# The root's reciprocal of fifteen normalisations computed as a power of -0.5 on GpSimd

## The chip, the cores and the metric

One core of one Trainium2 chip. The metric is the device time of one execution of the program in microseconds; the kernel before takes 1572.85 us (median of 3 runs, 1572.19 to 1574.05).

## The reference

Four layers run one after the other on x (16 sequences of 100 rows of 256 numbers) and a context (16 sequences of 361 rows). All of it is in float32. Cut to the normalisations, which alone are touched:

```
# layer 0: self attention, cross attention, feed-forward (gelu), a layer norm behind each
x = ln(x + self_attention(x));  x = ln(x + cross_attention(x, ctx));  x = ln(x + ffn(x))
#   ln(x) = (x - mean(x)) * rsqrt(var(x) + 1e-5) * gain + bias
# layer 1: self attention, swiglu, cross attention, swiglu, with residuals and without norms
# layer 2: rms(x) -> gates, a recurrence over 100 steps, attention on ctx; rms again -> gelu ffn
#   rms(x) = x * scale * rsqrt(mean(x * x) + 1e-6)
# layer 3: attention of the result on ctx, tanh of a product, added to the hidden states
```

## The kernel before

Activations lie transposed in SBUF, 256 features as two chunks (`DC`) of 128 partitions, 1600 columns for the 16 sequences. The columns are taken in four groups (`NG` = 4) of `GB` = 4 sequences, 400 columns each. The attention stages are called s0, c0 (layer 0), s1, c1 (layer 1) and c2 (layer 2), the feed-forward stages f0, f1, f2 and ft; they run in the order s0, c0, f0, s1, f1, c1, f2, gates, c2, ft, and then layer 3.

There are five normalisations of four groups each, 20 "chains": n1 (behind s0), n2 (behind c0), n3 (behind f0), r1 (ahead of layer 2) and r2 (ahead of ft). The chain of a group is spread over the stages that follow it: a product with a matrix of 1/256 gives the mean (n1 to n3), VectorE subtracts it (`dve_center`), ScalarE squares (`act_square`), a product gives the variance in PSUM (`pe_var`), ScalarE computes Sqrt of variance plus a small constant into `T2` (`act_root`), VectorE takes the reciprocal in place and multiplies both chunks (`dve_scale`), and for n1 to n3 ScalarE applies gain and bias (`act_affine`).

Each engine runs one list of instructions in order; semaphores are counted and each wait names a point that another engine marks. In an attention stage the order within a sequence is a string of tokens (`ORDER`). For c0 it is

```
"c0": "T0 T1 T2 n0 P1 n1 R0 R1 V0 R2 R3 T3 V1 T4 R4 R5 T5 F T6 T7 F K0 V2 K1 F X p0"
```

T is a score product of the next sequence and its maxima on VectorE (bank freed when the maximum is taken), R are the score products of this one and ScalarE's exponential (`act_probs`), X turns the maxima and VectorE makes `max_rows` of them (`dve_rows`), which the next sequence's R0 needs; F is one step of the "fill", among it the chain of the group before. With three F in a sequence of c0, the variance product and `act_root` of a chain lie in the first F of the group's third sequence, and `dve_scale` in its second F, ahead of that sequence's X on VectorE. In a feed-forward stage a fill step follows each of the eight hidden chunks (`pe_up`, then `act_evac` with the gelu), before the two products of `pe_down` that read all eight.

GpSimd (`program_pool`) runs `pool_masks` (one or two products of the queries with 0/1 columns; T needs the first, `qh`), in s0 also `pool_allowed`, in c1 and c2 sums of probabilities, and in c2 the steps of the recurrence. In c0 the masks of a sequence b wait for the last scores of sequence b - 3. T of sequence b + 1 is issued within sequence b.

ScalarE holds one set of function tables at a time; where the next function is in another, an ACT_TABLE_LOAD stands in its list.

Of the kernel before, what the change touches and what calls it, by code (L numbers as in the profile page):

```python
# [10 lines left out]
ACT = mybir.ActivationFunctionType  # L11
ALU = mybir.AluOpType
# [3 lines left out]
P = 128  # L16
DC = D // P
GB = 4
NG = B // GB
# [180 lines left out]
def build(nc, book, x_in, ctx_in, vec_in, const_in, src_in, w0_in, w1_in, w2_in, tw_in, out, spill):  # L200
    known = book.known
    with ExitStack() as ctx:
        def sb(name, shape, dt=F32):
            return ctx.enter_context(nc.sbuf_tensor(name, shape, dt))
# [23 lines left out]
        ONEB = sb("ones_bf", [P, P], BF16)  # L228
        ONES = sb("ones", [P, 64])
        IDB = sb("ident_bf", [P, P], BF16)  # L230
        EPS = sb("eps", [P, 2])
        PS = ctx.enter_context(nc.psum_tensor("psum", [P, 8, 512], F32))

# [66 lines left out]
        def mark(track, point, by=1):  # L301

            counts[track] += by
            book.marks[point] = (track, counts[track])
            book.totals[track] = counts[track]
            return by
# [4 lines left out]
        def at(point):  # L311
            return known.marks[point][1] if known else 0
# [14 lines left out]
        def bank(use):  # L327
            return known.banks[use] if known else 0
# [100 lines left out]
        def chain_earlier(n, g):  # L429

            i = CHAINS.index((n, g)) - 2
            return CHAINS[i] if i >= 0 else None

        def pe_terms(pe, ring, use, freed_by, terms, n=N, rows=P):

# [748 lines left out]
        def act_root(act, n, g):  # L1185
            if due(f"{n} var{g}"):
                act.wait_ge(products_ready, at(f"{n} var{g}"))
            eps = 0 if n[0] == "n" else 1
            nc.scalar.activation(T2[:, g % 2, 0, :], PS[:, bank(f"{n} var{g}"), 0:N], ACT.Sqrt, bias=EPS[:, eps:eps + 1]).then_inc(act_results, mark("act", f"{n} root{g}"))  # L1189

        def act_affine(act, n, g):
            gain, bias = GAIN[n]
# [419 lines left out]
                nc.vector.tensor_tensor(T1[:, g % 2, c, :], T1[:, g % 2, c, :], PS[:, bank(f"{n} mu{g}"), 0:N], ALU.subtract).then_inc(dve_results, mark("dve", f"{n} c{g} {c}"))  # L1612

        def dve_scale(dve, n, g):
            if due(f"{n} root{g}"):
                dve.wait_ge(act_results, at(f"{n} root{g}"))
            rs = T2[:, g % 2, 0, :]
            nc.vector.reciprocal(rs, rs).then_inc(dve_results, mark("dve", f"{n} rs{g}"))  # L1618
            if due(f"{n} rs{g}"):
                dve.wait_ge(dve_results, at(f"{n} rs{g}"))  # L1620
            for c in range(DC):
                if n in GAIN:
                    nc.vector.tensor_tensor(T1[:, g % 2, c, :], T1[:, g % 2, c, :], rs, ALU.mult).then_inc(dve_results, mark("dve", f"{n} t{g} {c}"))
                    continue
                if n == "r2" and g >= 2:
                    if due(f"ft f1{g - 2} 7"):
                        dve.wait_ge(products_ready, at(f"ft f1{g - 2} 7"))
                to, gain = (XN[g], "norm1") if n == "r1" else (T1[:, g % 2], "norm2")
                nc.vector.scalar_tensor_tensor(to[:, c, :], X[:, c, cols(g)], vec(gain, c), rs, ALU.mult, ALU.mult).then_inc(dve_results, mark("dve", f"{n} t{g} {c}"))
                mark_same(f"{'c2' if n == 'r1' else 'ft'} in{g} {c}", f"{n} t{g} {c}")  # L1630
# [259 lines left out]
        def program_dve(dve):  # L1890
            waited.clear()
            nc.vector.memset(ONEM[:, :], 1.0 / D).then_inc(dve_results, mark("dve", "p0"))
            nc.vector.memset(EPS[:, 0:1], 1e-5).then_inc(dve_results, mark("dve", "p1"))
            nc.vector.memset(EPS[:, 1:2], 1e-6).then_inc(dve_results, mark("dve", "p2"))
            nc.vector.memset(ONEB[:, :], 1.0).then_inc(dve_results, mark("dve", "p3"))
            nc.vector.memset(ONES[:, :], 1.0).then_inc(dve_results, mark("dve", "p4"))
            if due("vectors"):
# [86 lines left out]
        def pool_sum(pool, t, b, r):  # L1984
# [20 lines left out]
            nc.gpsimd.tensor_tensor(to, to, parts, ALU.add).then_inc(pool_results, mark("pool", f"{t} ds{b} {r}"))  # L2005
            mark_same(f"{t} ds{b}", f"{t} ds{b} {r}")

        def pool_steps(pool):

            for t in range(S):  # L2010
                if due(f"h{t - 1}"):
                    pool.wait_ge(dve_results, at(f"h{t - 1}"))
                if t == 0:
                    if due(f"gm{NG - 1}"):
                        pool.wait_ge(dve_results, at(f"gm{NG - 1}"))
                nc.gpsimd.tensor_tensor(ZH[t % 2], steps("zs", t), HC, ALU.subtract).then_inc(pool_results, mark("pool", f"zh{t}"))
                nc.gpsimd.tensor_tensor(HG[t % 2], steps("gms", t), HC, ALU.mult).then_inc(pool_results, mark("pool", f"hg{t}"))
                yield

        def program_pool(pool):  # L2020
# [9 lines left out]
            for b in range(B):  # L2030
# [5 lines left out]
                    pool_allowed(pool, "s0", b, r)  # L2036
                if b + 2 < B:
                    pool_masks(pool, "s0", b + 2)
            for t in ("c0", "s1"):
                for b in range(2 if t == "c0" else 0, B):  # L2040
                    pool_masks(pool, t, b)
            step = pool_steps(pool)
            for t in ("c1", "c2"):
                for b in range(2):
                    pool_masks(pool, t, b)
                for b in range(B):
                    for kind, n in tokens(t, b):
                        if kind == "S":
                            next(step, None)
                        elif kind == "a" and (t, b) != FINAL:  # L2050
                            pool_sum(pool, t, b, n)
                    if b + 2 < B:
                        pool_masks(pool, t, b + 2)
            for _ in step:
                pass

        def load_ctx(sp, b):
# [189 lines left out]
```

## Time and profile before

| | us |
|---|---|
| median of 3 runs | 1572.85 |
| the profiled execution, its own time | 1570.43 |
| its span, first to last instruction | 1568.7 |

| engine | busy us | share of the span | instructions |
|---|---|---|---|
| PE (matmul) | 1487.6 | 95% | 12256 |
| PEld (weight load) | 955.5 | 61% | 12256 |
| DVE (VectorE) | 773.3 | 49% | 1572 |
| ACT (ScalarE) | 668.8 | 43% | 1401 |
| POOL (GpSimd) | 263.6 | 17% | 443 |

The median granted TensorE clock is full but in short stretches; its mean over the span is 0.991. The engines' busy times are times between an instruction's start and its end; weight loads run beside matmuls. A timeline gives for each merged row its start and length in us, engine, line, operation, tiles and count, and in square brackets how long the engine had been idle before it and on whom it had waited.

### The profile page before, as it was taken

The numbers are of one execution on the slowest core, as the hardware profiler recorded it, in microseconds if no ns is written. First come the engines' busy times: TensorE is split into PE (matmuls) and PEld (weight loads), VectorE is DVE, ScalarE is ACT, GpSimd is POOL, SyncE is SP. The second block draws the span as 40 slices with busy tenths as digits, with TensorE's granted clock in tenths as the row PEclk, the third lists the DMA queues.
The fourth block names the chain that finished last, engine by engine and source line by source line (L and its number), as shares of the span: only waits on it lengthen the run. The fifth ranks groups of instructions, "written<-read, shape, count | busy, mean of one in ns | idle before, by whom it ended". The sixth has DMA issues, their size and how long they took to land.

```text
span 1568.7 us, 28764 instructions
## 1 busy us (share of the span) xinstructions
PE 1487.6 (95%) x12256; PEld 955.5 (61%) x12256; DVE 773.3 (49%) x1572; ACT 668.8 (43%) x1401; POOL 263.6 (17%) x443
## 2 busy tenths in 40 slices
PE   9888898998999999999999999999899999999998
PEld 8555565656555556555677765554566666655576
DVE  1677766867723156211233341333777777762132
ACT  2565556656545342111244331224554454443343
POOL 1433310010000000000022120000254454410000
PEclk9999999999989999999999999999999999999999
DMA  4321000000000020000100000000000000020032
GB/s 160 103 57 41 11 28 2 2 2 2 2 28 0 0 81 1 20 1 0 81 1 1 1 1 27 0 0 7 28 1 2 2 2 1 2 79 0 0 95 61
DMA packets 19562, 36.85 MB, mean 23 GB/s; under 512 B 2058, under 2 KB 17386, under 8 KB 18282
## 3 DMA queue, kind: packets, MB, share of 16 engines
q1 hardware_dynamic: 19434, 35.01, 6.7%
q8 instruction: 96, 1.57, 0.4%
q14 instruction: 32, 0.26, 0.1%
HBM read 33.36 MB, written 1.64 MB: 22 GB/s over the span
## 4 chain that ended last, share of the span: by engine, by line
PE 85%; DVE 9%; ACT 5%; issue 1%; DVEq 0%; ACTq 0%
PE psum L439 39%; PE psum L828 11%; PE psum L489 8%; PE psum L585 6%; PE psum L625 5%; DVE maxima L1508 3%; PE psum L581 3%; ACT probs L1168 3%; PE psum L524 2%; PE psum L933 2%; PE psum L961 1%; PE psum L942 1%; DVE t L1618 1%; PE psum L926 1%; PE psum L974 1%
## 5 line engine op out<-in xcount | busy, mean ns | idle before, releaser
L1508 DVE TENSOR_REDUCE maxima<-psum 100x2 f32<-100x722 f32 (+3 forms) x332 | 245.5, 760 | 111.1 <-PE psum L524 94.3
L439 PE MATMUL psum<-x_resid,weights 128*128 128x400 f32 x832 | 293.4, 503 | 3.6 <-ACT probs L1168 1.7
L439 PEld LDWEIGHTS psum<-x_resid,weights 128*128 128x128 f32 x832 | 156.5, 191 | 121.2 <-issue 3.8
L1168 ACT ACTIVATE probs<-psum 128x800 f32<-128x800 f32 (+3 forms) x224 | 168.0, 787 | 100.0 <-PE psum L585 99.7
L828 PE MATMUL psum<-weights 128*128 128x400 f32 x512 | 174.8, 499 | 0.7 <-DVE maxima L1508 0.7
L439 PE MATMUL psum<-weights,ctx_t 128*128 128x256 f32 (+1 forms) x576 | 155.6, 394 | 1.3 <-DVE max_rows L1519 0.7
L828 PEld LDWEIGHTS psum<-weights 128*128 128x128 f32 x512 | 97.3, 190 | 75.0 <-DVE maxima L1508 0.8
L489 PE MATMUL psum<-ctx_t,weights 128*128 128x361 f32 x384 | 137.5, 484 | 2.1 <-DVE weights L1739 0.8
L1090 ACT ACTIVATE weights<-psum 128x400 f32<-128x400 f32 (+2 forms) x80 | 37.9, 475 | 205.5 <-PE psum L439 205.4
L439 PEld LDWEIGHTS psum<-weights,ctx_t 128*128 128x128 f32 (+1 forms) x576 | 99.2, 184 | 41.2 <-issue 9.1
L625 PE MATMUL psum<-probs,values 128*32 128x100 f32 (+5 forms) x3328 | 112.9, 254 | 2.7 <-ACT q_then_o L1090 1.8
L1139 ACT ACTIVATE values<-psum 128x256 f32<-128x256 f32 (+2 forms) x176 | 67.7, 384 | 109.5 <-PE psum L439 74.5
L1966 POOL TENSOR_TENSOR q_masked_bf<-q_then_o,ones 128x200 bf16<-128x200 f32 x48 | 25.2, 528 | 510.4 <-ACT q_then_o L1090 448.1
L1739 DVE TENSOR_TENSOR weights<-psum,weights 128x400 f32<-128x400 f32 x64 | 36.8, 575 | 138.0 <-PE psum L439 119.7
L625 PEld LDWEIGHTS psum<-probs,values 128*32 128x32 f32 (+5 forms) x3328 | 85.9, 115 | 25.0 <-issue 19.4
L585 PE MATMUL psum<-q_masked,keys 32*128 32x200 f32 (+4 forms) x1408 | 97.3, 334 | 0.0
L489 PEld LDWEIGHTS psum<-ctx_t,weights 128*128 128x128 f32 x384 | 70.1, 194 | 35.1 <-issue 6.7
L1090 ACT ACTIVATE weights<-psum,vectors 128x400 f32<-128x400 f32 x80 | 46.2, 592 | 96.5 <-PE psum L439 95.4
L585 PEld LDWEIGHTS psum<-q_masked,keys 32*128 32x128 f32 (+4 forms) x1408 | 80.2, 181 | 0.1
L1519 DVE TENSOR_TENSOR max_rows<-psum,constants 128x400 bf16<-128x400 f32 (+1 forms) x80 | 39.0, 488 | 77.9 <-PE psum L555 77.3
L1618 DVE RECIPROCAL t<-t 128x400 f32<-128x400 f32 x20 | 53.0, 2648 | 45.9 <-ACT t L1189 45.9
L524 PE MATMUL psum<-keys_bf,q_masked_bf 32*100 32x361 bf16 (+1 forms) x448 | 66.3, 348 | 7.6 <-ACT probs L1168 4.0
(161 smaller groups left out, 2128.1 us busy)
## 6 DMA issues: line engine op xcount, KB each, us to landing
weights<-in_w SPq DMA_DIRECT2D x2, 3072.0 KB, 10.4
staged<-in_ctx SPq DMA_DIRECT2D x32, 128.0 KB, 2.1
values<-in_ctx SPq DMA_DIRECT2D x32, 128.0 KB, 2.1
weights<-in_w SPq DMA_DIRECT2D x3, 1024.0 KB, 4.5
weights<-in_src SPq DMA_DIRECT2D x1, 2368.0 KB, 14.5
weights<-in_w SPq DMA_DIRECT2D x1, 2048.0 KB, 7.7
weights<-in_tw SPq DMA_DIRECT2D x2, 1024.0 KB, 4.9
staged<-in_ctx SPq DMA_DIRECT2D x16, 105.0 KB, 2.2
```

What stands on the lines that cost most here:

```text
L439: i = nc.tensor.matmul(PS[0:rows, bk, 0:n], lhs, rhs, start=k == 0, stop=k == len(terms) - 1)
L489: i = nc.tensor.matmul(PS[:, bk + m, 0:C], w(WN[t][1], c, m * P, (m + 1) * P), CT[:, b, c, :], start=c == 0, stop=c == DC - 1)
L524: i = nc.tensor.matmul(PS[0:S, bk + d, 0:C], queries_bf(t, b, i0 + d, c, e), keys_bf(t, b, i0 + d, c, e), start=True, stop=True)
L581: nc.tensor.matmul(PS[0:kn, bk, 0:len(of) * n], ONEB[rows, 0:kn], maxima.unsqueeze(2).broadcast_to([a["tile"], c1 - c0, chunks, n]), start ...
L585: i = nc.tensor.matmul(PS[0:kn, bk, m * n:(m + 1) * n], keys_of(t, b, i0 + d, c, a["keys"][kc][0], kn), queries_of(t, b, i0 + d, c), start ...
L625: mm = nc.tensor.matmul(PS[head_rows(t, i, e), bk, o:o + S], lhs, probs_of(t, b, i, c, kc, kn, e), start=kc == 0, stop=kc == lastk)
L828: i = nc.tensor.matmul(PS[:, bk, 0:N], w(wd, k, m * P, (m + 1) * P), hidden[:, k, :], start=k == 0, stop=k == 7)
L1090: nc.scalar.activation(out, PS[0:rows, bank(use), 0:n], func, **kw).then_inc(act_results, mark("act", point or f"{use} out"))
L1139: nc.scalar.activation(dst, src, ACT.Copy).then_inc(act_results, mark("act", f"{use} out"))
L1168: nc.scalar.activation(PT[0:kn, k % PROBS_KEPT, :, 0:n], PS[0:kn, bk:bk + 2, 0:n], ACT.Exp).then_inc(act_results, mark("act", f"{t} p{b} { ...
L1508: nc.vector.reduce_max(top, src, AX).then_inc(dve_results, mark("dve", f"{t} m{b} {j}"))
L1618: nc.vector.reciprocal(rs, rs).then_inc(dve_results, mark("dve", f"{n} rs{g}"))
```

## The change

`by_power(n, g)` is true for n2, n3 and r1 (four groups each) and for r2's groups 1 to 3: 15 chains. For these `act_root` uses Identity in place of Sqrt, so that T2 holds variance plus constant; `pool_power` on GpSimd raises it in place to -0.5, a third column of `EPS` being the exponent, broadcast over the 400 columns; `dve_scale` has no reciprocal and waits for GpSimd. The powers stand in GpSimd's list so: those of n2's groups 0 to 2 behind the masks of c0's sequences 7, 11 and 15; n2's last and n3's first three behind all masks of c0; n3's last between the masks of s1's sequences 2 and 3; r1's four between c1 and c2; r2's three at the end.

```diff
-        EPS = sb("eps", [P, 2])
+        EPS = sb("eps", [P, 3])
...
+        def by_power(n, g):
+
+            return n != "n1" and (n, g) != ("r2", 0)
...
-            nc.scalar.activation(T2[:, g % 2, 0, :], PS[:, bank(f"{n} var{g}"), 0:N], ACT.Sqrt, bias=EPS[:, eps:eps + 1]).then_inc(act_results, mark("act", f"{n} root{g}"))
+            func = ACT.Identity if by_power(n, g) else ACT.Sqrt
+            nc.scalar.activation(T2[:, g % 2, 0, :], PS[:, bank(f"{n} var{g}"), 0:N], func, bias=EPS[:, eps:eps + 1]).then_inc(act_results, mark("act", f"{n} root{g}"))
...
         def dve_scale(dve, n, g):
-            if due(f"{n} root{g}"):
-                dve.wait_ge(act_results, at(f"{n} root{g}"))
             rs = T2[:, g % 2, 0, :]
-            nc.vector.reciprocal(rs, rs).then_inc(dve_results, mark("dve", f"{n} rs{g}"))
+            if not by_power(n, g):
+                if due(f"{n} root{g}"):
+                    dve.wait_ge(act_results, at(f"{n} root{g}"))
+                nc.vector.reciprocal(rs, rs).then_inc(dve_results, mark("dve", f"{n} rs{g}"))
             if due(f"{n} rs{g}"):
-                dve.wait_ge(dve_results, at(f"{n} rs{g}"))
+                dve.wait_ge(producer(f"{n} rs{g}"), at(f"{n} rs{g}"))
...
+            nc.vector.memset(EPS[:, 2:3], -0.5).then_inc(dve_results, mark("dve", "p5"))
...
+        def pool_power(pool, n, g):
+
+            if due(f"{n} root{g}"):
+                pool.wait_ge(act_results, at(f"{n} root{g}"))
+            rs = T2[:, g % 2, 0, :]
+            nc.gpsimd.tensor_tensor(rs, rs, EPS[:, 2:3].broadcast_to([P, N]), ALU.pow).then_inc(pool_results, mark("pool", f"{n} rs{g}"))
...
-            for t in ("c0", "s1"):
-                for b in range(2 if t == "c0" else 0, B):
-                    pool_masks(pool, t, b)
+            for b in range(2, B):
+                pool_masks(pool, "c0", b)
+                if b >= GB and b % GB == 3:
+                    pool_power(pool, "n2", b // GB - 1)
+            for n, g in [("n2", NG - 1)] + [("n3", g) for g in range(NG - 1)]:
+                pool_power(pool, n, g)
+            for b in range(3):
+                pool_masks(pool, "s1", b)
+            pool_power(pool, "n3", NG - 1)
+            for b in range(3, B):
+                pool_masks(pool, "s1", b)
             step = pool_steps(pool)
             for t in ("c1", "c2"):
+                if t == "c2":
+                    for g in range(NG):
+                        pool_power(pool, "r1", g)
...
             for _ in step:
                 pass
+            for g in range(1, NG):
+                pool_power(pool, "r2", g)
```

## Rows read from the trace of the kernel before

**Rows 1.** The page, part 1: busy us, share of the span, instructions of each engine.

```profile
PE 1487.6 (95%) x12256; PEld 955.5 (61%) x12256; DVE 773.3 (49%) x1572; ACT 668.8 (43%) x1401; POOL 263.6 (17%) x443
```

**Rows 2.** Line 1189 (`act_root`): duration ns min/median/max, first and last start, form.

```profile
L1189 ACT ACT_TABLE_LOAD  x20: 1283/1283/1283, 87.6 to 1452.4; - x20
L1189 ACT ACTIVATE t<-psum,eps x20: 593/593/594, 88.9 to 1453.7; 128x400 f32<-128x400 f32 x20
```

**Rows 3.** Line 1618 (the reciprocal), the same columns.

```profile
L1618 DVE RECIPROCAL t<-t x20: 2643/2644/2654, 90.0 to 1454.3; 128x400 f32<-128x400 f32 x20
```

**Rows 4.** Groups by line and form, GpSimd: busy us, mean ns, idle before.

```profile
L1971 POOL TENSOR_TENSOR q_masked<-q_then_o,constants 128x400 f32<-128x400 f32 x48 | 42.4, 884 | 0.0
...
L1971 POOL TENSOR_TENSOR q_masked_bf<-q_then_o,constants 128x400 bf16<-128x400 f32 x32 | 27.5, 859 | 212.7 <-PE psum L585 137.5 <-PE psum L524 53.5 <-ACT q_then_o L1090 21.7
```

**Rows 5.** Timeline of 288 to 326 us: stage c0, chain n2 of group 0.

```profile
292.57 0.35 PE L581 MATMUL psum<-max_rows,ones_bf 32*128 32x400 bf16 x4 [0.59 <-DVE maxima L1508]
...
301.27 0.59 ACT L1189 ACTIVATE t<-psum,eps 128x400 f32<-128x400 f32 x1
...
302.05 2.65 DVE L1618 RECIPROCAL t<-t 128x400 f32<-128x400 f32 x1
...
304.72 1.06 DVE L1623 TENSOR_TENSOR t<-t 128x400 f32<-128x400 f32 x2
305.05 0.51 PE L524 MATMUL psum<-keys_bf,q_masked_bf 32*100 32x361 bf16 x6
...
305.70 0.57 DVE L1519 TENSOR_TENSOR max_rows<-psum,constants 128x400 bf16<-128x400 f32 x1
306.19 2.53 DVE L1508 TENSOR_REDUCE maxima<-psum 100x2 f32<-100x722 f32 x3
...
308.05 0.35 PE L581 MATMUL psum<-max_rows,ones_bf 32*128 32x400 bf16 x4 [1.32 <-DVE maxima L1508]
```

**Rows 6.** Timeline of 414 to 448 us: the end of c0, chain n2 of group 2.

```profile
427.63 0.30 PE L555 MATMUL psum<-constants,maxima 100*128 100x100 f32 x1 [0.78 <-ACT values L1139]
...
431.86 0.35 PE L581 MATMUL psum<-max_rows,ones_bf 32*128 32x400 bf16 x4 [1.71 <-DVE max_rows L1519]
...
432.75 1.28 ACT L1168 ACT_TABLE_LOAD   x1
...
434.94 0.58 PE L581 MATMUL psum<-max_rows,ones_bf 32*105 32x400 bf16 x4 [2.05 <-ACT probs L1168]
```

**Rows 7.** Windows: length, busy us of PE, PEld, DVE, ACT, POOL, then the granted clock.

```profile
430.00:440.00 10.00, 5.21 (x77) 3.71 (x72) 4.51 (x10) 6.60 (x10) 0.00 (x0) 0.66 0.01 2
440.00:450.00 10.00, 10.00 (x114) 6.36 (x107) 2.83 (x6) 5.22 (x9) 0.00 (x0) 0.82 0.00 0
```

**Rows 8.** Timeline of 448 to 490 us: stage f0, chains n2 of group 3 and n3 of group 0.

```profile
471.19 0.59 ACT L1189 ACTIVATE t<-psum,eps 128x400 f32<-128x400 f32 x1 [9.35 <-PE psum L439]
...
475.11 1.33 ACT L1196 ACTIVATE x_resid<-t,vectors 128x400 f32<-128x400 f32 x2 [3.33 <-DVE t L1623]
...
479.83 1.58 PE L439 MATMUL psum<-t,ones_mean 128*128 128x400 f32 x4 [0.62 <-ACT t L1183]
...
485.28 5.20 PE L828 MATMUL psum<-weights 128*128 128x400 f32 x15
...
487.13 1.05 ACT L1090 ACTIVATE weights<-psum,vectors 128x400 f32<-128x400 f32 x2
```

**Rows 9.** Timeline of 540 to 580 us: the start of s1, chain n3 of group 3.

```profile
563.29 1.33 ACT L1196 ACTIVATE x_resid<-t,vectors 128x400 f32<-128x400 f32 x2 [2.94 <-DVE t L1623]
```

**Rows 10.** Timeline of 970 to 1016 us: stage f2, chain r1 of group 0.

```profile
987.17 1.22 DVE L1739 TENSOR_TENSOR weights<-psum,weights 128x400 f32<-128x400 f32 x2
...
990.23 10.91 PE L828 MATMUL psum<-weights 128*128 128x400 f32 x32
```

**Rows 11.** Timeline of 1040 to 1095 us: the start of the gates, chain r1 of group 3.

```profile
1073.59 0.61 PE L439 MATMUL psum<-vectors,weights 128*128 128x1 f32 x4 [0.91 <-ACT t L1189]
```

**Rows 12.** Timeline of 1416 to 1485 us: stage ft, the products of group 1.

```profile
1423.38 5.54 PE L439 MATMUL psum<-t,weights 128*128 128x400 f32 x16
```

## The prediction

> **What bounds the kernel now.** The page's first part comes first: TensorE is busy for 95% of the span and no other engine for more than 61% [rows 1]. So a saving on VectorE or ScalarE counts only where TensorE stands idle for it, and I looked next at the groups of lines 1189 and 1618 (each of 20 chains has one table load of 1.283 us, one Sqrt of 0.593 us, one reciprocal of 2.644 us [rows 2, 3]), then, in the timelines, at what TensorE does around each of the 15 chains. The reader is to see there that it waits in few of them: an extra 0.73 us in c0 for group 0 (the gap before R0 is 1.32 us in place of 0.59 us [rows 5]; group 1 looks the same), 0.78, 1.71 and 2.05 us at the end of c0, the last partly for a table load of the exponential [rows 6], 0.62 us in f0 [rows 8], 0.91 us at the gates [rows 11]. Behind the gaps of rows 6 the granted clock is 0.66 and 0.82 over two windows of 10 us, which is 3.4 + 1.8 = 5.2 us of full clock lost [rows 7]; elsewhere in these stretches TensorE runs at 2.4 GHz.
>
> **What goes.** ScalarE loses 15 loads at line 1189 and most of the loads that restore the table behind them: with 1.283 us each, some 29 loads or 37 us. VectorE loses 15 x 2.644 = 39.7 us. Nearly all lies beside TensorE's work. What it could bring at most, if the new operation cost nothing to wait for, is the sum of the gaps: 0.73 x 2, then 0.78 + 1.71 = 2.5 us at R0 of the last sequence, 2.05 down to about 0.85 = 1.2 us behind it, 5.2 us of clock, 0.6 us in f0, about 0.6 us for two short waits at the start of s1, and 0.5 of the 0.91 us at the gates (Identity starts without the 1.28 us load that overlapped the variance product): 12.1 us.
>
> The Trainium skill (ScalarE: Activation LUTs, Table sets: the hidden batching unit) has exp and sqrt in different sets and a load at about 2.7 us. The trace agrees on the two loads around a root, not on the size: 1.283 us. By 2.7 us the loads removed would be 78 us of ScalarE, still mostly hidden.
>
> **What comes: the power.** No row shows it, and everything hangs on its duration d. The nearest rows on GpSimd are products of the same size with a broadcast operand, 0.884 us [rows 4]; that is the lower end, as a power can't be less than a product. For the upper end I go by VectorE: there a reciprocal takes 2.644 us and a product of 400 columns 1.06 / 2 = 0.53 us [rows 3, 5], a factor of 5.0. The same factor on GpSimd gives 5.0 x 0.884 = 4.4 us for work as heavy as one division. A power is a logarithm, a product and an exponential; two such pieces give 8.8 us. Nothing bounds it above. I take the middle of the two, d = 6.6 us, an estimate: I think the power is nearer to the reciprocal than to the product. I keep 0.9 and 12 us for the range.
>
> **What the wait does, chain by chain, at d = 6.6.** The new wait stands on VectorE in `dve_scale`; behind it are the maxima rows of the next sequence (c0, s1), the centering (f0), the swiglu products (f2). ScalarE's affine step waits behind it with the gelus. On GpSimd the masks of the next sequence stand behind the power.
>
> - c0, groups 0 and 1. Without the load of 1.28 us ahead of it Identity runs about 300.1 to 300.7 (today from 301.27 for 0.59 us). Power until 307.4, two products until 308.5, `max_rows` (0.57) until 309.1, and the maxima start then instead of at 306.19 [rows 5]: 2.9 us later, twice, 5.8 us. Masks of sequence 8 end at 307.4 + 0.86 = 308.3 [rows 4], and T0, which ran at 305.05 [rows 5], follows: late too, but VectorE is later. Both are free up to d of about 2.8 to 3.3 us.
> - c0, group 2. Identity until 426.1, power until 432.8, products and rows until 434.5; R0 at 434.6 in place of 431.86: 2.7 us later. The table load at 432.75 is gone and with it 1.2 of the 2.05 us [rows 6]: net 1.5 us later. The low clock behind it stays.
> - f0, n2 of group 3. Root ends at 471.8; power to 478.5, first product 0.53, affine at 479.1 in place of 475.11: 4.0 us later, less the load of 1.28 us behind it. The variance product at 479.83, which waits for ScalarE already, comes 2.7 us later [rows 8].
> - f0, n3 of groups 0 and 1. The affine step comes 3.4 us later (4.0 less 0.6 of the load ahead), and with it the last two gelus, the first of which ends at 487.7. `pe_down` started at 485.28 and reads that chunk behind 12 of its 16 matmuls, at 5.20 / 15 = 0.35 us each, at 489.4 [rows 8]: 1.7 us of cover, 1.7 us lost. Group 1 has the same shape: 1.8 us. Group 2 has the opening of s1 behind it, more units and more banks: 0.5 us (0 to 3).
> - s1, n3 of group 3. Identity 1.28 us earlier; affine at 565.9 in place of 563.29 [rows 9], less the load of the exponential behind it (1.28): 1.3 us later.
> - f2, r1 of groups 0 to 2. VectorE would resume at 980.4 + 6.6 + 1.2 = 988.2, where the delayed swiglu products ran at 987.17 today, and the last one is read at 990.23 + 4.8 = 995 [rows 10]: nothing, up to d of about 11. Gates: 0.5 us earlier [rows 11]. ft, groups 1 to 3: power from about 1408.1, scaled at 1415.9, needed at 1423.38 [rows 12]: nothing, up to d of 14.
> - Clock. TensorE would stand idle for over 4 us in 6 us in both groups of c0; after comparable idling it fell to 1.2 GHz for a stretch [rows 6, 7]. I count a third of what rows 7 show, 1.7 us, for each: 3.4 us (0 to 10.4).
>
> Sum: 5.8 + 1.5 + 2.7 + 1.7 + 1.8 + 0.5 + 1.3 - 0.5 + 3.4 = 18.2 us. The profiled execution took 1570.43 us (span 1568.7 and 1.7 us around it), which gives 1588.6 us; it is 2.4 us below the median of the runs, so against the median 1572.85 + 18.2 = 1591.0 us.
>
> **The rivals.**
> 1. A short power (d up to 3.8 us). For it: a product takes only 0.884 us. Against: VectorE's own factor of 5. With d under 1.4 us all gaps above close: 12.1 us, 1560.8 us. At 3 us c0 still gains 0.5 us twice, R0 0.9 us, the exponential 1.2 us, s1 and gates 1.1 us: 5 us, 1568 us, and 1563 us where the low clock goes too. This ends on the other side; the turning point is d = 4.4 us. Chance 0.32.
> 2. Break-even (3.8 to 4.9 us). At 4.4 us: c0 0.7 x 2 later, its end 0.7 earlier, f0 0.5 later, s1 and gates 1.1 earlier: 0.1 us, 1573 us. Chance 0.13.
> 3. A heavy power (over 9 us). At 8.8 us the same terms are 10.2 + 3.7 + 4.9 + 7.9 + 2 + 3.5 - 0.5 and 7 us of clock: 38.7 us, 1611.6 us; every further us costs 7 chains 1 us each. Steps that don't overlap, 20 passes at the product's 0.884 us, would be 18 us and over 1670 us. Chance 0.22. The Trainium skill (GPSIMD Engine Reference, Performance pitfalls for Q7 kernels) has 4 cycles an element for each dependent float32 step, which would be this case; no row here shows it.
>
> That loads stay, so that ScalarE saves nothing, I count within these: the keys' Identity follows a Sqrt today without a load, so the new one should not need one.
>
> **How the numbers follow.** Forecast (4.9 to 9 us) 0.33, rivals 0.32, 0.13, 0.22. Range: 1561 us is the most that can be gained; upward half of the heavy case is left out, d of about 12: 1611.6 + 3.2 x 7 = 1634 us. From 1561 to 1634 about 0.13 is left out. The slower cases alone lie from 1576 to 1634. Faster by over 0.2% (3.1 us, about what a measurement can tell from no change) 0.32, within it 0.13, slower 0.55.
>
> **What would show it.** The duration of the new TENSOR_TENSOR at `pool_power`: under 3.8 us I am wrong on the sign. The gap before R0 of c0's sequences 7 and 11 should be over 3 us in all, spread over T0 and R0; maxima at 309.1 and not 306.2. The variance product in f0 should wait some 3 us. ScalarE should have some 29 table loads fewer. In f2 and ft nothing should move. Clock stretches at half speed should appear in c0's groups 1 and 2. If the power is 6.6 us and the time doesn't move, then the covers are larger than I read them.

## The result: the time rose by 877 us, and the profile after

The kernel after takes 2449.68 us (median of 4 runs, 2447.77 to 2450.5) against 1572.76 us beside it: 1.558 times as long, 95% interval 1.5563 to 1.56. The forecast was 1591.0 us in a range of 1561 to 1634. The sign was right, the size was not: +877 us in place of +18.

The page of the kernel after, its first two parts (busy time of each engine; the span in 40 slices) and two rows of its groups (line, engine, operation, shapes, count, busy us and mean ns, idle time before and on whom):

```profile
PE 1524.9 (62%) x12256; PEld 973.0 (40%) x12256; DVE 736.5 (30%) x1558; ACT 632.4 (26%) x1372; POOL 1226.2 (50%) x458
...
PE   9889909181701441369999993532359999912469
...
POOL 2340091929389668730002218669744444389830
PEclk9999959585855765779999997866679999956679
...
L2020 POOL TENSOR_TENSOR t<-t,eps 128x400 f32<-128x400 f32 x15 | 961.5, 64098 | 375.3 <-ACT t L1194 375.3
```

One power takes 64.1 us. TensorE's share of the span fell from 95% [rows 1] to 62%, and its slices are empty where GpSimd's are full: little overlaps any more. Fifteen powers are 961.5 us, and the program is 877 us longer; the difference is taken apart behind the table below.

The same stretch of c0 as [rows 5], in the timeline of the kernel after:

```profile
303.30 64.10 POOL L2020 TENSOR_TENSOR t<-t,eps 128x400 f32<-128x400 f32 x1 [34.82 <-ACT t L1194]
...
367.37 0.85 POOL L1978 TENSOR_TENSOR q_masked_bf<-q_then_o,constants 128x400 bf16<-128x400 f32 x1
367.43 2.36 DVE L1629 TENSOR_TENSOR t<-t 128x400 f32<-128x400 f32 x2 [62.78 <-POOL t L2020]
368.18 1.19 POOL L1978 TENSOR_TENSOR q_masked<-q_then_o,constants 128x400 f32<-128x400 f32 x1
368.27 0.84 PE L528 MATMUL psum<-keys_bf,q_masked_bf 32*100 32x361 bf16 x6 [60.63 <-POOL q_masked_bf L1978]
...
372.06 0.52 PE L585 MATMUL psum<-max_rows,ones_bf 32*128 32x400 bf16 x4 [0.79 <-DVE maxima L1513]
```

TensorE stops at T0, because the masks of the next sequence stand behind the power on GpSimd; then R0 still waits 0.79 us for VectorE's maxima. Both routes of the forecast are there. Two smaller things are new: VectorE's two products take 2.36 us in place of 1.06 [rows 5] while GpSimd makes masks beside them, and one of these masks takes 1.19 in place of 0.86 us [rows 4].

The windows of that stretch (us, busy time of PE, PEld, DVE, ACT, POOL with counts, granted clock, DMA):

```profile
304.00:368.00 64.00, 3.64 (x58) 2.44 (x57) 1.22 (x2) 2.30 (x5) 64.00 (x2) 0.57 0.00 0
368.00:376.00 8.00, 6.93 (x82) 4.78 (x86) 7.46 (x12) 3.79 (x7) 3.32 (x4) 0.50 0.01 2
```

The clock falls to half during the wait and is still there for the first 8 us of work behind it. The same happens at each of the 15 waits; the clock stays low for 3 to 12 us behind them, which adds up to 38 us of full clock lost. That fits TensorE's busy time, which grew by 37.3 us (1487.6 to 1524.9) for the same 12256 matmuls.

Where each wait ended, one row of a place (TensorE's timeline of the kernel after; rows of several windows):

```profile
621.67 0.52 PE L585 MATMUL psum<-max_rows,ones_bf 32*128 32x400 bf16 x4 [61.90 <-DVE max_rows L1524]
...
729.64 3.00 PE L443 MATMUL psum<-t,ones_mean 128*128 128x400 f32 x4 [60.67 <-ACT t L1187]
...
799.96 9.07 PE L832 MATMUL psum<-weights 128*128 128x400 f32 x20 [59.26 <-ACT weights L1094]
...
971.21 4.75 PE L443 MATMUL psum<-x_resid,weights 128*128 128x400 f32 x8 [60.50 <-ACT q_then_o L1094]
...
1062.29 3.04 PE L443 MATMUL psum<-x_resid,weights 128*128 128x400 f32 x4 [60.37 <-ACT q_then_o L1094]
...
1632.87 9.71 PE L832 MATMUL psum<-weights 128*128 128x400 f32 x22 [52.45 <-DVE weights L1745]
...
1801.32 4.39 PE L443 MATMUL psum<-staged,weights 128*128 128x400 f32 x8 [56.21 <-DVE staged L1635]
...
2270.80 7.86 PE L443 MATMUL psum<-t,weights 128*128 128x400 f32 x16 [50.05 <-DVE t L1635]
```

64.1 us less such a gap, corrected by the gap that stood there before, is the cover of that place, and it can be set beside the cover that the forecast read (its d of 6.6 us less the loss that it counted at 6.6 us):

| place | gap after, less gap before | cover measured | cover by the forecast |
|---|---|---|---|
| c0, groups 0 and 1 | 60.63 + 0.79 - 1.32 = 60.1 | 4.0 | 3.7 |
| end of c0, R0 | 61.90 - 1.71 = 60.2 | 3.9 | 3.9 |
| f0, variance of n2 group 3 | 60.67 - 0.62 = 60.05 | 4.05 | 3.9 |
| f0, n3 group 0 (group 1 alike) | 59.26 | 4.8 | 4.9 |
| n3 group 2 | 60.50 | 3.6 | 6.1 |
| s1, n3 group 3 | 60.37 | 3.7 | 5.3 |
| f2, three groups | 52.45 | 11.65 | 11 |
| gates | 56.21 - 0.91 = 55.3 | 8.8 | none given |
| ft, three groups | 50.05 | 14.05 | 14 |

The covers are 119 us in all (8.0 + 3.9 + 4.05 + 9.6 + 3.6 + 3.7 + 35 + 8.8 + 42.2). 961.5 - 119 is 842 us of new waits; the other 35 of the 877 us are about the 37 us that the clock added to TensorE's busy time, less a few us that the change gives back. Of the eight places with a forecast five were read right (within 0.2 us, in f2 within 0.7). The number that was wrong by a factor of ten is d.

That c0 agrees as well (4.0 and 3.7) is luck. The forecast's 3.7 us is 6.6 us less the lateness of the maxima, and with them of R0. R0 stood at 308.05 [rows 5] and now stands at 372.06, and TensorE's list was 2.5 us later than before already ahead of the power: R0 is 61.5 us late, and the cover is 64.1 - 61.5 = 2.6 us. The two gaps are shorter than this lateness, because T0 between them ran at half clock (0.84 us in place of 0.51) and so did the value products. The 2.6 us can be worked out: the reciprocal ended at 304.7 [rows 5], the power starts at 303.3 - 2.5 = 300.8 on the same count, which is 3.9 us, and VectorE's two products are 1.3 us longer. At the end of c0, where no mask follows the power, the cover is 3.9 us.

ScalarE did what was said. Its groups of table loads in the kernel after are 7 + 7 + 5 + 1 = 20, where there were 49:

```profile
L1094 ACT ACT_TABLE_LOAD x7 | 9.0, 1283 | 6.7 <-PE psum L443 6.6
L1172 ACT ACT_TABLE_LOAD x7 | 9.0, 1283 | 1.6 <-PE psum L589 1.5
L1194 ACT ACT_TABLE_LOAD x5 | 6.4, 1283 | 0.1
L1384 ACT ACT_TABLE_LOAD x1 | 1.3, 1283 | 0.0
```

### The profile page after: what moved, and what is told of

It reads as the page before. It is cut to its first block, busy times and chain, and to the rows that moved or that the text cites. A ratio compares the mean times of both kernels' runs of the same rounds, so it can differ in the third digit from the quotient of the medians.

```text
span 2447.9 us, 28739 instructions
## 1 busy us (share of the span) xinstructions
PE 1524.9 (62%) x12256; PEld 973.0 (40%) x12256; DVE 736.5 (30%) x1558; ACT 632.4 (26%) x1372; POOL 1226.2 (50%) x458
## 4 chain that ended last, share of the span: by engine, by line
PE 49%; POOL 37%; DVE 6%; ACT 3%; POOLq 3%; issue 2%; DMA 0%; SPq 0%; DVEq 0%; ACTq 0%
POOL t L2020 37%; PE psum L443 22%; PE psum L832 5%; PE psum L493 5%; PE psum L589 4%; PE psum L629 3%; POOLq L202 3%; DVE maxima L1513 2%; PE psum L585 2%; ACT probs L1172 2%; PE psum L528 1%; PE psum L937 1%; PE psum L965 1%; PE psum L946 1%; PE psum L930 1%
## 5 line engine op out<-in xcount | busy, mean ns | idle before, releaser
L2020 POOL TENSOR_TENSOR t<-t,eps 128x400 f32<-128x400 f32 x15 | 961.5, 64098 | 375.3 <-ACT t L1194 375.3
L832 PE MATMUL psum<-weights 128*128 128x400 f32 x512 | 186.1, 522 | 276.5 <-DVE weights L1745 157.4
L1629 DVE TENSOR_TENSOR t<-t 128x400 f32<-128x400 f32 x24 | 15.6, 693 | 529.2 <-POOL t L2020 529.1
L443 PE MATMUL psum<-t,weights 128*128 128x400 f32 x176 | 70.6, 550 | 151.1 <-DVE t L1635 151.1
L1201 ACT ACTIVATE x_resid<-t,vectors 128x400 f32<-128x400 f32 x24 | 16.2, 715 | 504.8 <-DVE t L1629 504.8
L2007 POOL TENSOR_TENSOR staged<-probs 128x400 f32<-128x400 f32 x46 | 47.4, 1030 | 145.5 <-ACT probs L1172 145.5
L443 PEld LDWEIGHTS psum<-weights,ctx_t 128*128 128x128 f32 (+1 forms) x576 | 100.1, 186 | 42.1 <-issue 10.2
L1635 DVE SCALAR_TENSOR_TENSOR t<-x_resid,vectors,t 128x400 f32<-128x400 f32 x12 | 7.1, 632 | 338.0 <-POOL t L2020 337.9
L443 PEld LDWEIGHTS psum<-t,weights 128*128 128x128 f32 x176 | 35.7, 209 | 179.9 <-DVE t L1635 152.0
L2030 POOL TENSOR_TENSOR scan_state<-weights,h_parts 128x32 f32<-128x32 f32 x100 | 27.2, 272 | 155.7 <-DVE h_parts L1843 106.6
```

What stands on the lines that cost most here:

```text
L443: i = nc.tensor.matmul(PS[0:rows, bk, 0:n], lhs, rhs, start=k == 0, stop=k == len(terms) - 1)
L832: i = nc.tensor.matmul(PS[:, bk, 0:N], w(wd, k, m * P, (m + 1) * P), hidden[:, k, :], start=k == 0, stop=k == 7)
L2020: nc.gpsimd.tensor_tensor(rs, rs, EPS[:, 2:3].broadcast_to([P, N]), ALU.pow).then_inc(pool_results, mark("pool", f"{n} rs{g}"))
```

## Experiments

The runs of before beside them gave 1571.5 to 1571.7 us, so a difference is taken against these and not against 1572.85. "Products by ones" is the instruction of the change with another operation, so that queues and waits stay while its duration is chosen. "Place by place" means how much later or earlier TensorE's list stands at a point than in the kernel before, from one profiled execution of each. Short stretches of low clock come and go there without any of the change's waits beside them: one in c2 (from 1126 us in the kernel before) costs 2.4 us and is missing in several of the runs, one in c0 costs 1.6 us in the first run below. This is why single terms are read together with the ratio.

### A cheap step: one product

```diff
-            nc.gpsimd.tensor_tensor(rs, rs, EPS[:, 2:3].broadcast_to([P, N]), ALU.pow)
+            nc.gpsimd.tensor_tensor(rs, rs, ONES[:, 0:1].broadcast_to([P, N]), ALU.mult)
```

> The change as it stands, with the power on GpSimd replaced by one product with a column of ones (so the scale factor is variance plus constant, not its inverse root). The work around it, the waits and the lists are those of the change; only the duration d of the new step falls from 64.1 to about 0.88 us. Theory A, that only d was wrong in the prediction and the covers and gaps were read rightly: all gaps that the chains leave on TensorE close, 12.1 us less than before, 1560.7 us; without the return of the clock in c0's last stretch (5.2 us) 1566. Theory B, that the waits and the order on GpSimd cost something by themselves: no gain or a loss, 1573 or more. GpSimd's products 0.88 us each.

Measured: 1561.88 us, ratio 0.9939 (0.9924 to 0.9954), 9.8 us less. TensorE's timeline at the end of c0, where [rows 6] are the kernel before:

```profile
427.92 0.31 PE L559 MATMUL psum<-constants,maxima 100*128 100x100 f32 x1 [0.78 <-DVE maxima L1513]
...
430.37 0.35 PE L585 MATMUL psum<-max_rows,ones_bf 32*128 32x400 bf16 x4
430.55 0.85 PE L589 MATMUL psum<-q_masked,keys 32*128 32x200 f32 x16
432.33 0.38 PE L585 MATMUL psum<-max_rows,ones_bf 32*105 32x400 bf16 x4 [0.93 <-ACT probs L1172]
```

Against before, the wait of 1.71 us is gone, 2.05 us became 0.93, 0.78 stayed, and the matmuls behind run at full clock. Place by place: c0 -0.73 twice, its end with the low clock behind it -5.8, f0 -0.9, s1 -0.9, gates -0.56, together -9.6 us. So the rest of the change works as described, and is worth 0.6% when the step costs 0.85 us.

### Each half alone

Only the loads go (the kernel before with Identity for the 15 roots, reciprocal kept):

```diff
-            nc.scalar.activation(..., ACT.Sqrt, bias=EPS[:, eps:eps + 1])
+            nc.scalar.activation(..., ACT.Identity if n != "n1" and (n, g) != ("r2", 0) else ACT.Sqrt, bias=EPS[:, eps:eps + 1])
```

> The kernel before with Identity in place of Sqrt in the 15 chains and nothing else: table loads go, the reciprocal of 2.64 us stays on VectorE, GpSimd is as before. (The inverse root becomes an inverse.) Theory A, in which the reciprocal in front of max_rows makes the gaps of c0: the 0.73 us gaps stay, the gap before the exponential at the end of c0 (2.05 us) shrinks by about 1.2, R0 there comes some 0.6 to 1.3 earlier, f0, s1 and the gates give 0.6 + 0.6 + 0.5: 3.5 to 4 us less, 1569 us, and up to 5 more if the clock doesn't fall. Rival, that the loads are what costs: nearly all of what the run with one product gains.

Only the reciprocal goes (the one-product kernel with its root kept):

```diff
-            func = ACT.Identity if by_power(n, g) else ACT.Sqrt
+            func = ACT.Sqrt
```

> As the run with one product on GpSimd, but with Sqrt kept on ScalarE, so the table loads stay and only the reciprocal has left VectorE. (The factor is the root, not its inverse.) Theory A: c0 gains 0.73 us twice and about 1.7 us at its end, f0 0.6: 3.5 to 4 us less, 1569 us; the clock may or may not fall. Rival, that loads are what costs: within 1 us of 1572.8. The gains of this run and of the one with Identity alone should not simply add: each leaves the other's wait in place at the end of c0.

Measured: without the loads 1564.77 us, 0.9966 (0.995 to 0.9983); without the reciprocal 1569.19 us, 0.9978 (0.9966 to 0.9989). Place by place: the end of c0 gains 2.2 us without the loads and 2.6 without the reciprocal, f0 0.9 us by either (with both gone it gains no more), s1 1.0 and 0.4, the gates 0.56 and nothing. c0's 0.73 us needs both: with the loads alone gone nothing moved there, with the reciprocal alone gone 0.25 us a group, where 0.73 was expected. The two intervals overlap, so which half is worth more overall stays open.

### The forecast's own case: seven products, 6.44 us

```diff
+            for k in range(7):
+                if k:
+                    if due(f"{n} part{g} {k - 1}"):
+                        pool.wait_ge(pool_results, at(f"{n} part{g} {k - 1}"))
+                nc.gpsimd.tensor_tensor(rs, rs, ONES[:, 0:1].broadcast_to([P, N]), ALU.mult).then_inc(...)
```

> The change with seven products by ones, one behind the other, in place of the power: d of 7 x 0.88 plus the waits between them, 6.2 to 7 us, about the 6.6 us of the prediction (the factor is again variance plus constant). It tests the sum of the prediction at its own d. Theory A, that the covers were read rightly: 18.2 us more than before, 1591 us, with the clock term of 3.4 us (0 to 10.4) its least certain part; maxima in c0 2.9 us late, the variance product in f0 2.7 us late, nothing in f2 and ft. Theory B, that the covers are deeper than read (the queues ahead absorb it): under 1580 us.

Measured: 1602.88 us, ratio 1.0196 (1.0177 to 1.0215), 31.3 us more. The timeline of c0's group 0:

```profile
304.84 6.44 POOL L2024 TENSOR_TENSOR t<-t,ones 128x400 f32<-128x400 f32 x7 [34.82 <-ACT t L1194]
...
311.24 0.85 POOL L1978 TENSOR_TENSOR q_masked_bf<-q_then_o,constants 128x400 bf16<-128x400 f32 x1
311.31 2.35 DVE L1629 TENSOR_TENSOR t<-t 128x400 f32<-128x400 f32 x2 [5.13 <-POOL t L2024]
...
312.14 0.84 PE L528 MATMUL psum<-keys_bf,q_masked_bf 32*100 32x361 bf16 x6 [2.97 <-POOL q_masked_bf L1978]
...
315.93 0.52 PE L585 MATMUL psum<-max_rows,ones_bf 32*128 32x400 bf16 x4 [0.78 <-DVE maxima L1513]
```

and three windows of it:

```profile
300.00:311.00 11.00, 9.02 (x97) 5.53 (x96) 4.47 (x6) 6.05 (x11) 5.69 (x7) 1.00 0.01 1
311.00:321.20 10.20, 8.27 (x98) 5.99 (x100) 8.02 (x12) 4.14 (x7) 4.18 (x5) 0.50 0.01 2
321.20:331.00 9.80, 8.50 (x107) 5.35 (x101) 5.04 (x6) 5.70 (x10) 1.66 (x2) 1.00 0.01 2
```

TensorE's new idle time for one group is 2.97 + 0.78 - 1.32 = 2.4 us, but the clock is at half from 311.0, inside the first gap, for 10.2 us, and the group costs 6.3 us. Of that 3.9 us are the clock's, where the forecast had 1.7. R0 itself is 3.8 us late (315.93, less the 4.1 us that the list had been later, against 308.05), where the forecast had 2.9: the cover is 2.6 us again. With a gap of 2.85 us for n3's group 2 the clock falls too:

```profile
563.86 3.51 PE L443 MATMUL psum<-x_resid,weights 128*128 128x400 f32 x5 [2.85 <-ACT q_then_o L1094]
```

(+4.7 us at that place, forecast 0.5), and in s1, here behind two rows of the kernel before:

```profile
564.53 0.48 ACT L1090 ACTIVATE q_then_o<-psum 128x400 f32<-128x400 f32 x1
565.03 1.28 ACT L1168 ACT_TABLE_LOAD   x1
```

```profile
597.04 2.35 PE L443 MATMUL psum<-x_resid,weights 128*128 128x400 f32 x4 [2.69 <-ACT q_then_o L1094]
```

(+4.1 us, forecast 1.3). Both times TensorE waits for ScalarE's copy of the queries, which stands right behind the affine step in ScalarE's list. In s1 the load that goes stands behind that copy, so the 1.28 us which the forecast took off for it shorten nothing here.

The other places came out as forecast: end of c0 +1.6 (1.5), variance of n2 group 3 +2.4 (2.7), n3 groups 0 and 1 +1.9 each (1.7 and 1.8), gates -0.56, f2 and ft nothing. All places together are 28 us. The profiled execution, the slowest of four, stands 4 us late by the first 10 us of the program, ahead of everything that was changed; so up to 3 of the 31.3 us may not be the step's.

### Two points around the break-even: four and five products

The same edit with 4 and 5 products (3.65 and 4.58 us).

> The step on GpSimd as four products by ones (4 x 0.92 = 3.7 us), so the kernel computes the norms without the root's reciprocal. Theory of the prediction: covers and gains as read, break-even at a duration of 4.4 us; at 3.7 us c0's two groups lose 0.5 us each, all else still gains: about 1569 us. Theory with the collision: in c0 the two products on VectorE take 2.35 us in place of 1.06 beside GpSimd's masks, so the loss there is 6.4 - 1.7 (low clock) less 2.8 us = 1.9 us for each group; end of c0 -0.8 us, f0 -0.4, gates -0.6, s1 -1.0, n3 0: a sum of about +1, 1573 us. Under 1570 us speaks for the first.

> The same with five products (5 x 0.92 = 4.6 us). Theory of the prediction: 0.2 us past its break-even of 4.4 us, times some 8 us of program for each us of the step: 1573.5 us. Theory with the collision: c0 +2.8 us twice (1.7 us more each if the clock falls again), its end +0.1, f0's variance product of n2 +0.1, n3 of group 2 +1.0 and s1 +0.5 us, gates -0.6: about +6.7, 1578.5 us, or 1582 us with the clock.

Measured: four 1572.03 us, 1.0008 (0.9998 to 1.0019); five 1581.99 us, 1.0063 (1.0048 to 1.0078). Both agree with the account that has the collision on VectorE and low clock, and not with the forecast's break-even at 4.4 us; it lies near 3.6. With four products, c0's group 1, which kept full clock, costs 1.03 us, and group 0, with 3.4 us of low clock behind it, 2.65. Five products, timeline of c0's group 0:

```profile
302.92 4.58 POOL L2024 TENSOR_TENSOR t<-t,ones 128x400 f32<-128x400 f32 x5 [34.82 <-ACT t L1194]
...
307.53 2.35 DVE L1629 TENSOR_TENSOR t<-t 128x400 f32<-128x400 f32 x2 [3.27 <-POOL t L2024]
...
308.37 0.51 PE L528 MATMUL psum<-keys_bf,q_masked_bf 32*100 32x361 bf16 x6 [1.11 <-POOL q_masked_bf L1978]
...
312.15 0.52 PE L585 MATMUL psum<-max_rows,ones_bf 32*128 32x400 bf16 x4 [2.10 <-DVE maxima L1513]
```

1.11 + 2.10 - 1.32 = 1.9 us of waiting at full clock, so the cover is 4.58 - 1.9 = 2.7 us here, 1.0 less than the forecast read. TensorE waits for VectorE at the end, and VectorE's products are 1.3 us longer than in [rows 5]. By the lateness of R0 (1.04, 1.96 and 3.8 us with four, five and seven products, 61.5 with the power) the cover is 2.6 us in all four kernels. By the gaps it looks like 4.0 us behind a long wait (6.44 - 2.4, and the kernel after): TensorE's own work ahead of R0 then runs at half clock and fills part of VectorE's delay.

### Is it the masks on GpSimd? Masks ahead of the step

Seven products again; GpSimd issues the masks of c0's sequences 8 and 12 ahead of the step instead of behind it.

```diff
-                if b >= GB and b % GB == 3:
-                    pool_power(pool, "n2", b // GB - 1)
+                if b > GB and b % GB == 0:
+                    pool_power(pool, "n2", b // GB - 2)
+            pool_power(pool, "n2", NG - 2)
```

> The run with seven products (d of 6.44 us, 1602.9 us) with one edit: on GpSimd the masks of c0's sequences 8 and 12 stand ahead of the step of n2's groups 0 and 1 instead of behind it. In the run with seven products these chains cost 6.3 and 6.4 us each: a wait of 2.97 us of T0 for the masks, two products on VectorE that took 2.35 us together beside GpSimd's masks instead of 1.06, and a stretch of half clock. Theory A: VectorE and GpSimd hinder each other there and the long idle stretch brings the clock down. With the masks early T0 doesn't wait, the products take 1.06 us, the maxima start some 1.2 us earlier; 1.2 us twice less without the clock, about 3 us twice less with it: 1597 to 1600 us. Theory B: the wait of VectorE for the step alone sets the time, the masks are not to blame: same as the run with seven products, 1603 us.

Measured: 1599.85 us, ratio 1.0183 (1.0169 to 1.0197); the intervals of this and the seven products overlap. The timeline of its c0, group 0:

```profile
305.31 0.51 PE L528 MATMUL psum<-keys_bf,q_masked_bf 32*100 32x361 bf16 x6
...
307.54 2.35 DVE L1629 TENSOR_TENSOR t<-t 128x400 f32<-128x400 f32 x2 [5.14 <-POOL t L2024]
308.27 1.19 POOL L1978 TENSOR_TENSOR q_masked<-q_then_o,constants 128x400 f32<-128x400 f32 x1
...
312.15 0.52 PE L585 MATMUL psum<-max_rows,ones_bf 32*128 32x400 bf16 x4 [5.16 <-DVE maxima L1513]
```

T0 waits no more, and all of the wait has moved to R0, which is 3.8 us late as with seven products; the two groups cost 6.2 and 6.5 us in place of 6.3 and 6.4. So VectorE's list sets the time in c0, and GpSimd's queue behind the step does not. The median is 3.0 us lower, as the other theory had it, but c0 has at most 0.2 us of that; the profiled execution of the seven products lost more in the first 10 us of the program (4.1 against 0.3 us). My idea that the products would also shrink to 1.06 us fell, since the masks of the sequence after that now stand behind the step and run beside them just the same.

### What the power costs: its size and exponent

The power kept, on parts of the tile, with other rows, columns and exponents; the rest of the columns stays unnormalised.

```diff
+            rows, cols_of, power = SHAPES[n, g]
+            part = T2[0:rows, g % 2, 0, 0:cols_of]
+            nc.gpsimd.tensor_tensor(part, part, EPS[0:rows, power:power + 1].broadcast_to([rows, cols_of]), ALU.pow).then_inc(...)
```

> The change with the power on a part of the tile, another part in each chain (the rest of the columns or rows is not raised): in n2 128 rows and 100, 50, 10 and 1 columns; in n3 100 columns and 16, 8, 1 and 64 rows; in r1 100 columns with exponents -1, 2 and 1, then 200 columns with -0.5; in r2 100, 50 and 20 columns. Theory 1, a cost per column and none for the rows: 64.1 / 400 = 0.160 us a column, so 16.0 us for 100, 8.0 for 50, 1.6 for 10, 32 for 200, and 16.0 us for every number of rows. Theory 2, the lanes of a GpSimd core are computed one after another: 16 rows as 128, 8 rows 8 us, 1 row 1 us for 100 columns. Theory 3, a fixed start of tens of us (code loaded): 1 column costs nearly as much as 400. Exponents: a general power takes 16.0 us for each; special cases would show as shorter for 1, 2 or -1. The whole, by theory 1 and covers of 3.5 us in c0, 4.8 in f0 and s1, 8 at the gates and 11.6 in f2: about 100 us of waits less some 8 gained, 1668 us.

Measured, one run: 1696.33 us. GpSimd's groups, form by form:

```profile
L2030 POOL TENSOR_TENSOR t<-t,eps 128x100 f32<-128x100 f32 x5 | 81.6, 16315 | 154.1 <-ACT t L1200 154.1
...
L2030 POOL TENSOR_TENSOR t<-t,eps 128x200 f32<-128x200 f32 x1 | 32.2, 32236 | 16.6 <-ACT t L1200 16.6
...
L2030 POOL TENSOR_TENSOR t<-t,eps 1x100 f32<-1x100 f32 x1 | 16.3, 16295 | 21.3 <-ACT t L1200 21.3
...
L2030 POOL TENSOR_TENSOR t<-t,eps 128x10 f32<-128x10 f32 x1 | 2.0, 1951 | 31.5 <-ACT t L1200 31.5
L2030 POOL TENSOR_TENSOR t<-t,eps 128x1 f32<-128x1 f32 x1 | 0.5, 548 | 37.9 <-ACT t L1200 37.9
```

The step is a straight line: (32.236 - 16.315) / 100 = 0.159 us for each column and about 0.4 us beside; 400 columns give 64.1 us. One row costs what 128 do, and exponents of -1, 2 and 1 cost 16.31 to 16.33 us for 100 columns, as -0.5 does. Nothing is saved by a simpler exponent, and no start-up is paid on the first one. The whole came out 28 us over what was expected. The expectation had no term for the clock, and TensorE's busy time is 22.5 us longer than before (1510.1 against 1487.6).

### Other ways to the same end, on ScalarE

Logarithm, then exponential of -0.5 times it, for n1 and n2 (e^(-0.5 ln v) is the root's reciprocal), and, in a second kernel, for c0's four groups alone:

```diff
+                nc.scalar.activation(rs, PS[:, bank(f"{n} var{g}"), 0:N], ACT.Ln, bias=EPS[:, eps:eps + 1]).then_inc(...)
+                nc.scalar.activation(rs, rs, ACT.Exp, scale=-0.5).then_inc(...)
```

> Another way to the same aim, without GpSimd: for n1 and n2 (8 chains) ScalarE computes exp(-0.5 ln(variance + constant)) in two steps and VectorE has no reciprocal; n3, r1, r2 as before. Each chain has a load for the logarithm and one for the exponential, the second of which serves the probabilities behind it: no more loads than before in s0 and c0. From root to scale: load 1.28 + 0.59 against the reciprocal's 2.65, about 0.8 us shorter. Theory A: the 0.73 us gaps in c0 close (four, n1's last among them), at its end R0 comes 0.9 us earlier and the exponential waits for no load (1.2 us): 4 to 5 us less, 1568 us, and up to 5 more if the clock doesn't fall there. Rival: ScalarE's own list is later by 1.9 us a chain before keys and values, and that costs TensorE as much: 1573 us or more.

> As the run with logarithm and exponential on ScalarE, but only for the four chains that lie in c0 (n1's last, n2's first three), where exponentials follow anyway. Theory A: the gain of that run came from c0 alone (the 0.73 us gaps and the end of the stage), its 0.84 us in f0 is given back: 3 us less than before, 1569 us. Rival: s0's three chains lost something there, and without them the gain is larger, 1567 us or less.

Measured: 1568.47 us, 0.9978 (0.9969 to 0.9987), and 1571.58 us, 1.0001 (0.9992 to 1.001). ScalarE's timeline of the first:

```profile
300.70 1.28 ACT L1195 ACT_TABLE_LOAD   x1
302.00 0.59 ACT L1195 ACTIVATE t<-psum,eps 128x400 f32<-128x400 f32 x1
302.61 1.28 ACT L1198 ACT_TABLE_LOAD   x1
303.90 0.54 ACT L1198 ACTIVATE t<-t 128x400 f32<-128x400 f32 x1
```

The logarithm needs a load and the exponential behind it another, although the exponential is what ScalarE had computed just before. c0's 0.73 us is won three times (n1's last chain lies there too), but keys and values behind the chain come later and cost 1.06 us each time; the gain is at the end of c0. The second kernel should have kept the gain of the first (1569 us was expected) and didn't. In the profiled executions the two stand alike up to the end of c0 (1.1 and 1.4 us ahead of the kernel before); then the first gains 0.8 us in f0, and the second loses 2.4 us in c2, where its clock is low for 13.7 us (from 1123 us) and that of the kernel before for 6.8. That is the stretch which comes and goes. Why its 11 runs lie as high as those of the kernel before is not shown.

The root's reciprocal as one ScalarE function, for all 20 chains, nothing on GpSimd:

```diff
-            nc.scalar.activation(T2[:, g % 2, 0, :], PS[:, bank(f"{n} var{g}"), 0:N], ACT.Sqrt, bias=EPS[:, eps:eps + 1])
+            nc.scalar.activation(rs, PS[:, bank(f"{n} var{g}"), 0:N], ACT.Abs_reciprocal_sqrt, bias=EPS[:, eps:eps + 1])
...
-            nc.vector.reciprocal(rs, rs)
```

> The kernel before with ScalarE's Abs_reciprocal_sqrt in place of Sqrt in all 20 chains and no reciprocal on VectorE; GpSimd as before. One instruction gives the inverse root; it has a table of its own, so the loads stay. Theory A, from the run that kept Sqrt but took the reciprocal away (2.5 us less): the same gains in c0 and f0, and n1's last chain and r2's first with them, where the products wait for VectorE: 3 to 5 us less than before, about 1568 us. Rival, a load or the function itself takes longer than for Sqrt: over 1571 us.

Measured: 1565.54 us, ratio 0.9965 (0.995 to 0.9979), 6.0 us less than before. It beats the kernels before and after; only kernels that leave out part of the root's reciprocal were faster. Place by place the chains give 5.8 us: 0.25 for each of three groups in c0, its end 2.6, f0 0.9, s1 0.4 and ft, whose first chain the change had left alone, 1.15. ScalarE's groups in it:

```profile
L1195 ACT ACT_TABLE_LOAD x20 | 25.7, 1283 | 0.4
...
L1195 ACT ACTIVATE t<-psum,eps 128x400 f32<-128x400 f32 x20 | 11.9, 593 | 15.9 <-PE psum L443 15.8
```

It takes 593 ns, what the Sqrt took [rows 2], and needs as many loads; what it saves is VectorE's 2.64 us in each chain [rows 3].

## Why the forecast was wrong, step by step

- **What bounds the kernel and what goes**: right. 29 loads fewer, and with a cheap step 9.8 us gained where at most 12.1 were counted. Two terms were too large: the gap of 0.78 us stayed, and the low clock at the end of c0 was put at 5.2 us, where the place shows 5.8 us in all, of which 1.71 + 1.12 = 2.8 are gaps, so some 3 us of clock. TensorE isn't busy all through such a stretch (5.21 of the first 10 us [rows 7]). f0 and s1 gave 0.3 us each beyond what was counted.
- **The duration of the power**: the step that failed. It was scaled: GpSimd's product 0.884 us, times the factor of 5.0 between reciprocal and product on VectorE, then doubled. The product's row bounds a power from below and nothing bounds it from above, as the text said itself; the middle of two values that were both made from a product says nothing of a function whose cost no row showed. Measured, the ratio to the product is 64.1 / 0.884 = 73, not 7.5. Rival 3 had the right direction, a step far heavier than a product, but stopped at 20 passes (over 1670 us), and its chance of 0.22 was cut again for the range, of which only the part up to 12 us was kept.
Either the rule does not bear on this instruction or the count of operations, which was a guess, is a tenth of what runs; no run here tells the two apart.
- The same skill has a change of table set at about 2.7 us (ScalarE: Activation LUTs, Table sets: the hidden batching unit); its section What ACT_TABLE_LOAD costs splits this into a load of about 1.28 us and a drain of about 1.38 us. The runs agree on where loads stand and on the load, 1.283 us for each of the 20 left. No such drain shows: between Ln and Exp, in the kernel with both, 303.90 - 302.59 = 1.31 us pass in all.
- **The covers, chain by chain**: right in five of eight places (table above), at 64.1 us as at 6.44. n3's group 2 was put at 6.1 us of cover "for more units and more banks" without rows of its own, and has 3.6; s1 was put at 5.3, by taking off a load that stands behind what TensorE waits for, and has 3.7. In c0 the cover is 2.6, not 3.7: the two products collide with the masks. The forecast took 1.06 us for them from a row in which GpSimd was idle, though it said that the masks would start right behind the power.
- **The clock**: mis-sized. A third of [rows 7], 1.7 us, was counted for each group of c0; with 6.44 us it measured 3.9, and n3's group 2 and s1, which had none, lost 1.8 and 1.4 us beside their gaps. With the two covers, and less the 1.0 us by which c0's idle time came out shorter, they make up 10 of the 13 us between 31.3 and 18.2 in the forecast's own case (clock 4.4 + 3.2, gaps of the two places 2.35 + 1.4); the other 3 us lie outside the places. In all, each further us of the step costs (1602.9 - 1582.0) / (6.44 - 4.58) = 11 us of the program in this range, where 7 to 8 were counted.
- **The turning point**: 3.6 us in place of 4.4, by these two causes. With the true d neither matters for the sign.

## What to carry to other kernels

When everything hangs on an operation that no row shows, the range has to be as wide as the ignorance: a product's row times a guessed factor is no upper end, and one instruction of the wanted operation, timed by itself, is worth more than the rest of the sum. The other terms can be read well from the gaps and covers of the trace, if each duration is taken from a row with the same neighbours beside it, and if each new wait of some us is charged for the clock behind it too. An idle engine is no reason to give it work; compare what one instruction costs there, and first look for a function that the engine already in the chain can compute at the same price.

## What the runs showed of the hardware

- A float32 power on GpSimd: 0.159 us for each column, whatever the rows (1, 8, 16, 64, 128) and the exponent (-1, -0.5, 1, 2), and 0.4 us beside. 128x400 takes 64.1 us, a product of the same tile 0.85.
- VectorE's two products of 128x400 take 2.35 us beside a GpSimd product and 1.06 us without; GpSimd's mask then takes 1.18 in place of 0.85 us. Both engines pay.
- TensorE's clock: in waits of 50 to 62 us it was at half speed but for their start, and 3 to 12 us on; with the 2.97 us gap of the seven-product kernel for 10.2 us, from inside the gap; behind 1.11 and 2.10 us with five products for 3.4 us, behind 2.1 us with four once the same and once not at all.
- On ScalarE Abs_reciprocal_sqrt costs the 593 ns of a Sqrt and one load of 1.283 us; Ln followed by Exp costs two loads.
